# A software-pipelined RWKV layer with top-1 experts: x plus x1 moved to VectorE, a turn's scatter moved into the next step, and channel keys from an input mixed on ScalarE and GpSimd

## The reference, cut to what matters

```python
h = _ln(x, ln1_g, ln1_b); h1 = _time_shift(h)
k, v, r = mix(h, h1, mix_k) @ tm_Wk, mix(h, h1, mix_v) @ tm_Wv, mix(h, h1, mix_r) @ tm_Wr
x1 = x + (sigmoid(r) * _wkv(k, v, -exp(time_decay), time_first)) @ Wo     # time mixing
h = _ln(x1, ln2_g, ln2_b); h1 = _time_shift(h)
xk = h * cm_mix_k + h1 * (1.0 - cm_mix_k)                                  # channel mixing
xr = h * cm_mix_r + h1 * (1.0 - cm_mix_r)
kc = square(relu(xk @ cm_Wk))
out = x1 + sigmoid(xr @ cm_Wr) * (kc @ cm_Wv)
x = _layernorm(x + out)
top1 = argmax(softmax(x @ router_w + router_b))        # the expert of each token
```

## Time and profile before

| what | value |
|---|---|
| time, median of 3 runs | 707.67 us (706.49 to 709.01) |
| the profiled execution: time | 706.2 us |
| the profiled execution: span of the records | 704.5 us |
| PE, DVE, ACT, POOL busy over the span | 89%, 67%, 52%, 40% |
| step -2 to 8 and the tables, until the first product of the experts | 0 to 234.6 us |
| experts | 234.6 to about 350 us |
| second layer | about 350 to 704.5 us |

### The profile page before, as it was taken

One profiled execution on the slowest core, in us unless ns is written; L12 is line 12 of the kernel. 1 busy time (PEld: TensorE's weight loads), 2 busy tenths in 40 slices (PEclk: granted clock), 3 DMA queues, 4 the chain that ended last, 5 costly groups with the idle time before them and its releaser, 6 DMA issues. The chain is left out here.

```text
span 704.5 us, 14982 instructions
## 1 busy us (share of the span) xinstructions
PE 630.2 (89%) x4107; PEld 521.4 (74%) x4108; DVE 471.4 (67%) x1534; ACT 366.8 (52%) x818; POOL 284.2 (40%) x558
## 2 busy tenths in 40 slices
PE   4599989998781799999878899999999999999995
PEld 3488888888671799999734677877777777787773
DVE  5799988988724255445336577777877777777642
ACT  4489877788541344444212455545555455444542
POOL 1444877787555311111144343334443344332201
PEclk9699999999895699999999999999999999999999
DMA  5071112210112677777200000000000000000000
GB/s 146 30 243 60 48 37 67 74 60 16 54 45 88 216 240 228 240 240 234 60 19 9 8 8 9 16 15 15 15 15 15 15 8 11 11 16 8 9 8 15
DMA packets 39458, 46.99 MB, mean 67 GB/s; under 512 B 5184, under 2 KB 31104, under 8 KB 39424
## 3 DMA queue, kind: packets, MB, share of 16 engines
q1 hardware_dynamic: 35520, 39.50, 17.7%
q0 software_dynamic: 3328, 6.82, 3.5%
q10 hardware_dynamic: 576, 0.26, 0.1%
HBM read 34.58 MB, written 7.80 MB: 60 GB/s over the span
## 5 line engine op out<-in xcount | busy, mean ns | idle before, releaser
L449 PE MATMUL banks<-xg_cols,w 128*128 128x128 f32 x624 | 78.7, 281 | 0.3 <-ACT xg_cols L483 0.3
L449 PEld LDWEIGHTS banks<-xg_cols,w 128*128 128x128 f32 x624 | 75.4, 198 | 0.7 <-issue 0.7
L507 DVE SCALAR_TENSOR_TENSOR hidden<-banks,b_cols,gate 128x128 f32<-128x128 f32 x156 | 43.9, 344 | 45.9 <-ACT gate L476 45.9
L476 ACT ACTIVATE gate<-banks,b_cols 128x128 f32<-128x128 f32 x156 | 44.5, 368 | 56.0 <-PE banks L449 56.0
L1507 PE MATMUL banks<-ffn_w,act_cols 128*128 128x128 f32 x512 | 66.2, 278 | 0.7 <-ACT act_cols L1658 0.7
L1507 PEld LDWEIGHTS banks<-ffn_w,act_cols 128*128 128x128 f32 x512 | 60.6, 192 | 7.9 <-issue 6.4
L1501 PE MATMUL banks<-slots_cols,ffn_w 128*128 128x512 f32 x128 | 64.1, 606 | 0.8 <-ACT slots_cols L1673 0.8
L533 POOL DMA_DIRECT2D xg<-sorted_x x40 | 21.9, 546 | 80.8 <-PE banks L458 63.6
L1658 ACT ACTIVATE act_cols<-banks 128x512 f32<-128x512 f32 x64 | 38.2, 597 | 28.2 <-PE banks L1501 28.2
L627 PE MATMUL banks<-consts,normed 128*128 128x128 f32 x96 | 20.6, 301 | 28.2 <-ACT normed L800 28.2
L1724 POOL TENSOR_TENSOR rstd_b<-mean_var_b,eps 128x2 f32<-128x2 f32 x16 | 3.1, 195 | 105.0 <-DVE mean_var_b L1793 105.0
(11 more groups left out here) (244 smaller groups left out, 1622.0 us busy)
## 6 DMA issues: line engine op xcount, KB each, us to landing
w<-w_dram SPq DMA_DIRECT2D x39, 512.0 KB, 4.4
xg<-sorted_x POOLq DMA_DIRECT2D x40, 64.0 KB, 3.8
sorted_y<-y_rows SPq DMA_DIRECT2D x39, 64.0 KB, 3.2
x_in_rows<-x_dram SPq DMA_DIRECT2D x16, 128.0 KB, 2.1
x_res<-x_dram SPq DMA_DIRECT2D x16, 128.0 KB, 2.1
xa<-normed SPq DMA_DIRECT2D x16, 128.0 KB, 2.2
stage<-normed SPq DMA_DIRECT2D x16, 128.0 KB, 2.1
out_dram<-final SPq DMA_DIRECT2D x16, 128.0 KB, 1.8
```

What stands on the lines that cost most here:

```text
L449: last = pe.matmul(bank(u, k, c * P, (c + 1) * P), w1[parity][u][:, lo:lo + P], xg_cols[u][:, :], start=True, stop=True)
L476: act.activation(gate[u][:, c, :], bank(u, 2, c * P, (c + 1) * P), ACT.Sigmoid, bias=b1_cols[:, bass.ds(e1 * GC + XC + c, 1)]).then_inc(ga ...
L507: last = dve.scalar_tensor_tensor(hidden[u][:, c, :], bank(u, 1, c * P, (c + 1) * P), b1_cols[:, bass.ds(e1 * GC + c, 1)], gate[u][:, c, : ...
```

## The change

Four things change in the first part of the program.

The channel keys: ScalarE evicts the transposed `normed2` twice more (`key_parts`), once multiplied by the mixing factor and once by one minus it, GpSimd adds the two, the second shifted by a token, into `key_cols`, and TensorE makes each key by one product with the plain weights. `h2_cols` is still made, later, for the receptance.

`x01` is made on VectorE from `x_res` times two plus the product in PSUM (`sum_with_input`), at the end of the step. TensorE waits for it before it transposes over the same bank.

`find_places` and `scatter` of a turn come in the next step, split around the norm's scales. The last turn scatters from `normed3` and slots of its own.

The orders on all engines are rewritten; the slots' norms of the second layer move to the front of step 7, and a Sigmoid is evaluated once before the experts.

```diff
-                        mixed_columns(dst, h2_cols[u], "cm_Wk", k * P, (k + 1) * P).then_inc(R["kc_ready"][u], 1)
+                        pe.matmul(dst, cm_wk[:, k * P:(k + 1) * P], key_cols[u][:, :], start=True, stop=True
+                                  ).then_inc(R["kc_ready"][u], 1)
...
                     def time_receptance(u):
+                        pe.wait_ge(R["h1_ready"][u], m + 1)
...
                         pe.wait_ge(R["normed2_ready"][u], c * NT + NT)
+                        pe.wait_ge(R["x01_ready"][u], c + 2)
                         turn(bank(u, 0), normed2[u], R["turned2"][u])
...
                     def first_keys(u):
-                        pe.wait_ge(R["h2_ready"][u], c + 1)
+                        pe.wait_ge(pool_rwkv[3], c * (U + 3 * U) + u + 1)
...
                     def other_keys(u):
+                        if "R" in parts:
+                            pe.wait_ge(R["xa_cols_ready"][u], r + 1)
...
+                        time_receptance(0)
                         keys_and_values(0)
-                        time_receptance(0)
...
                     if "R" in parts:
+                        token_logits(0)
+                    if "C" in parts:
+                        other_keys(1)
+                    if "R" in parts:
                         token_logits(1)
                     if "C" in parts:
-                        other_keys(1)
                         channel_values(0)
...
+                    def key_parts(u):
+                        act.wait_ge(R["turned2"][u], c + 1)
+                        act.activation(key_now[u][:, :], bank(u, 0, 0, T), ACT.Identity,
+                                       bias=key_mix[:, 1:2], scale=key_mix[:, 0:1])
+                        act.activation(key_before[u][:, 1:T + 1], bank(u, 0, 0, T), ACT.Identity,
+                                       bias=key_mix[:, 3:4], scale=key_mix[:, 2:3]).then_inc(R["h2_ready"][u], 1)
...
-                    if "M" in parts:
-                        for u in range(U):
-                            pool.wait_ge(R["x1_ready"][u], m + 1)
-                            pool.tensor_tensor(x01[u][:, :, :], x_res[u][:, :, :], x1[u][:, :, :], ALU.add
-                                               ).then_inc(R["x01_ready"][u], 1)
...
+                    if "R" in parts and "C" in parts and follows(r):
+                        find_places(r - 1)
+                    if "C" in parts:
+                        for u in range(U):
+                            pool.wait_ge(R["h2_ready"][u], c * 2 + 1)
+                            p3.step(pool.tensor_tensor(key_cols[u][:, :], key_now[u][:, :], key_before[u][:, 0:T],
+                                                       ALU.add))
+                    if "R" in parts and "C" in parts and follows(r):
+                        scatter(r - 1, 0)
...
-                    dve.wait_ge(scattered, 16 * TURN_TILES * (TURNS - 1))
-                    dve.tensor_copy(slot_now[:, :], last_place[:, :]).then_inc(slots_ready, 1)
+                    dve.tensor_copy(last_slots[:, :], last_place[:, :]).then_inc(slots_ready, 1)
...
+                def sum_with_input(u):
+                    dve.scalar_tensor_tensor(x01[u][:, :, :], x_res[u][:, :, :], 2.0, by_rows(bank(u, 0, 0, T)),
+                                             ALU.mult, ALU.add).then_inc(R["x01_ready"][u], 1)
```

230 lines of the change are left out of this document (131 added, 99 removed).

## The result

The changed kernel takes **716.86 us** (median of four runs, 714.9 to 717.17) against 707.61 for the kernel before on the same chip (706.49 to 709.01): ratio **1.0124**, 95% interval 1.0098 to 1.015. It is slower, and above the predicted range of 700 to 714 us. The profiled execution has a span of 715.5 us, 11.0 more than before, and a mean granted clock of 0.952 instead of 0.961.

What follows compares the result with a forecast made beforehand. Prediction: a step was bound by GpSimd's list in its first half, PE in its second. From the profiled 706.2, +1.3 +4.5 -4.5 gave 707.5; the runs' median lies 1.5 above, so 709.0 us, range 700 to 714.

Steps and rivals of the forecast that it cites:

- Steps 1 to 6: Loop term: 23.5 us a step (23.3 to 23.8), 141.0 against 136.5, so +4.5 us (ends +3.0 and +6.6).
- (a): Chain in a step, from the end of `mean_var` through GpSimd's scales and `normed` to ScalarE's next instruction: 2.43 us, unchanged.
- (b): Chain on ScalarE from there to `xa_cols` of the second sequence, with four key parts added: 8.90 becomes 10.57 us.
- (c): Chain through `xa_cols`, two keys and the logits on PE, with gaps between engines: 1.95 us.
- (d): Chain on VectorE from `logits` to the end of `mean_var`: 8.36 us; a `y_cols` collision with GpSimd could add 0.53.
- Up to step 0: Start term: receptance ahead of the first keys, two sums on VectorE and a wait for `keep_state`: +1.3 us (+0.5 to +1.8).
- rival of a falling clock: Slower rival: TensorE idles and its clock falls in the loop, 2 us a step for five steps, 719 us; 10 in 100.
- The sum on VectorE: Moving `x01` to VectorE: 0.34 us twice, off the chain behind `mean_var`; 1.3 us given back to VectorE worth nothing.
- The drain: From the end of step 6's `mean_var` to the experts' first product, 46.4 us before: -4.5 us (-2.5 to -6.5).
- 8 products fewer: Drain gain: eight products fewer in step 7, half of which ran at half clock, 4.9 us.
- the 2.5 for the slots' rows: Drain gain: VectorE takes the last logits without first waiting on the slots' rows, which waited for GpSimd: 2.5 us.
- Sigmoid: Sigmoid ahead of the experts: PE is busy 10.67 of 11.00 us in the stretch with its table load, so worth nothing.

Runs made afterwards that it cites:

- e2: The changed kernel with the first sequence's keys and values ahead of its receptance on TensorE and the four `key_mix` operations behind the weights' mixing: ratio 1.0083.
- e1: The changed kernel with keys and values of the first sequence ahead of its receptance again in TensorE's order: ratio 1.0128.
- e7: e2 with ScalarE's key parts of the second sequence behind the kept shares of the first instead of ahead of them: ratio 1.0138.
- e4: The changed kernel with channel keys made by two products again, without key parts, GpSimd's key sums and the `key_mix` operations at the start: ratio 1.0056.
- e17: e2 with x plus x1 made on GpSimd again, as the last thing of its step: ratio 1.0088.
- e11: The kernel before with x plus x1 made on VectorE instead of GpSimd, nothing else: ratio 0.9901.
- e3: The kernel before with the last turn scattered from the normalised rows with its own slots, and GpSimd's slot scale ahead of the last step's first scatter: 702.86 us, ratio 0.9939.
- e6: e2 with the slot rows' squares behind the last channel gate, their scale behind the last norm, and the slot rows at the step's end: ratio 1.0082.
- e15: e9 with the sigmoid's table loaded ahead of the experts, as in the changed kernel: ratio 0.9846.
- e10: e9 with the channel keys by one product from input mixed on ScalarE and GpSimd: ratio 1.0072.
- e9: The kernel before with e3's drain edits, x plus x1 on VectorE, and a turn's places and scatter in the next step: 696.4 us, ratio 0.984.
- e12: e10 with each key product made twice, the second overwriting the first; the traced step takes 23.69 us against 23.68 in e10.

## Why the prediction was wrong

The forecast was +1.3 us on the profiled execution, and it was +11.0. Of the 9.7 us between them, 5.3 lie up to step 0, 2.5 in the drain and 2.1 in steps 1 to 6 (0.2 come back behind the drain). The sum's terms, in the order of the prediction:

- *Steps 1 to 6*: 141.0 forecast, 143.1 measured (58.02 to 201.09). The chain was right, and term by term. In step 3, (a) from the end of `mean_var` to ScalarE's next instruction takes 2.60 us (2.43 forecast), (b) ScalarE's stretch to `xa_cols` 10.58 (10.57), (c) from there to VectorE's last logits 1.93 (1.95), (d) VectorE's stretch to the end of `mean_var` 8.50 (8.36, and a part of the 0.53 for `y_cols`, which does take 0.95). Steps 2 to 5 take 23.6 (forecast 23.5, 23.3 to 23.8); step 1 takes 23.47, 1.9 more than before, where steps 2 to 5 grew by 0.5. Of the 2.1 us over the forecast 1.6 are step 6, 25.20 at a granted clock of 0.86 where e2's step 6 takes 23.64 at 1.00. There the channel values of the first sequence ran at half clock, 3.76 us instead of 2.05:
```profile
192.23 3.76 PE L702 MATMUL banks<-cm_wv,k_sq 128*128 128x128 f32 x16
```
  The ends +3.0 and +6.6 do not follow from 23.3 and 23.8 us, which give +3.3 and +6.3.
- *Up to step 0*: **the step that failed**. +1.3 forecast (at most +1.8), +6.6 measured. "The four small instructions for `key_mix` lie behind the first load" was wrong: they stand ahead of the first statistics and put them 0.8 us later, at no price in the sum. In the traces of e1 and e2 this is 2.0 us at the end of step -1 and 2.8 with step 0; 0.9 of it is there also where the clock rises equally late (e7), the rest came with a later rise that is not shown to be the edit's. The next 1.7 us are the keys' in step 0 (23.38 in e2, 21.73 in e4): after the key products TensorE waits 2.75 us for the squares, and its channel values then take 3.37 us instead of 1.95, as the rows of the changed kernel show:
```profile
49.42 3.37 PE L702 MATMUL banks<-cm_wv,k_sq 128*128 128x128 f32 x16 [2.75 <-ACT k_sq L884]
...
54.28 1.95 PE L702 MATMUL banks<-cm_wv,k_sq 128*128 128x128 f32 x16
```
  The term also took the wrong engine for the full one. It has "VectorE, without pause in step 0", but before the change VectorE waited 2.07 and 1.21 us there for TensorE's products, and TensorE was busy in all of the 21.04 us:
```profile
30.39:51.43 21.04, 21.04 (x124) 18.77 (x123) 17.11 (x44) 16.44 (x39) 8.47 (x19) 0.96 0.68 215
```
  In the changed kernel TensorE has less work in step 0 (19.70 us) and waits 4.5 us in it, 1.71 for ScalarE ahead of the keys and the 2.75 above. That wait is in no term of the sum.

  My rival of a falling clock put such slow products into the loop and priced it at 2 us a step; in the changed kernel it came in steps 0, 1 and 6. The channel values of step 0 took 1.4 us longer by it, step 6 took 1.6, and step 1 nothing. So the price was near where the slowed products are the channel values, and the count was wrong. The receptance ahead of the first keys, which I charged 0.9 for, costs nothing (e1). Together 4.4 of the 6.6 us lie between traces that differ by an edit; the other 2.2 no run assigns, and executions with the same start differ by 1.2 us there.
- *The sum on VectorE*: nothing, forecast and measured (e17), in the changed kernel. The reason given, that VectorE waits for ScalarE there anyway, fits. What the prediction never priced is the edit without the keys: on the kernel before it is worth 1.4 us a step (e11), about the 1.3 that it worked out and set aside.
- *The drain*: -4.5 forecast (-2.5 to -6.5), -2.0 measured. Its two gains were right by themselves, e3 gives -3.7. The squares and scales ahead of the first key were sized right: 209.26 is 7.9 us behind the end of `mean_var`, 191.59 was 3.4 behind it, so 4.5 late for 4.7 forecast. What I mis-sized is the "8 products fewer", 4.9: from the first key product to the end of the last it is 7.5 us instead of 11.3, so 3.8; and the channel values start 1.4 us later than before, counted from `mean_var`, the last statistics of the third norm come 2.0 later, and the last logits reach VectorE 29.55 us behind `mean_var` (230.64), where they came at 29.5 before (217.37, two merged). So nothing of the 2.5 for the slots' rows arrived. With the squares back the drain is 3.1 shorter (e6).
- *Sigmoid*: nothing, right (e15).

The forecast of "lost in the loop, won in the drain" had the right shape. What its form hid is the size of the keys' cost: the chain was compared only with the step of the kernel before, 23.06, and came out 0.4 above it. Compared with the kernel before less GpSimd's sum, 21.6, the same chain costs 2 us. Nor are the keys the only thing that keeps a step long: with two products again the rewritten orders take 23.3 (e4), with one product the old orders take 23.7 (e10), and both together 23.6. Either of the two is enough to lose what the sum's move wins, and taking back one of them alone gives back little in the loop.

## What to carry to other kernels

Price each edit of a bundle on its own against the others: here one was worth -7 us, one -4.5 and one +16, and the sum of my terms showed +1.3. An engine that feeds the full ones has less slack than its busy time says: ScalarE was busy 18.1 of 21.6 us (e9), and 1.97 us more on it made the step 1.6 us longer. And look at what stands ahead of the first consumer of the first load: 0.8 us there was still 0.9 at the end of step -1, and more where the clock rose later too. One trace is not enough to price the start: executions with the same program up to there lay 1.2 us apart.

## What the runs showed of the hardware

- TensorE's clock did not rise at a fixed distance behind its first product, and not at one that the program alone sets: 5.8 us in the changed kernel (9.44 to 15.25), 3.2 in e2 (8.65 to 11.89), and 5.8 again in e7 (8.73 to 14.54), whose program is e2's up to there.
- The clock can fall in a step and cost nothing: e6 has 0.93 in each of its steps 2 and 3, which take 23.6 as the others. Keeping it up can win nothing: e10 at 0.93 and e12 at 1.00 both take 23.7. The Trainium skill, TensorE: Matmul & The Clock Gate, HAM oscillation, warns of bursts between waits; the traces agree that the clock falls there, and show that the cost differs: nothing in those steps, 1.6 us in the changed kernel's step 6, where the channel values were the slowed products.
- A VectorE sum of 128x512 takes 2.00 us beside two GpSimd sums of 128x256, and 0.69 alone. Taking the 1.42 us of sums off GpSimd made a step 1.4 us shorter, 1.3 of it in that one VectorE instruction.
